# A two-layer transformer block with sorted experts: clearing fewer rows of the sorted array, on another queue

## What is computed

```
xn = layernorm(x)
x  = x + linear_attention(xn) + moe16(xn)     # 16 experts of 176, every token weighed over its best 6
xn = layernorm(x)
x  = x + recurrence(xn) + moe8(xn)            # scan of 512 steps: s = tanh(u_t + s*gamma + beta)
                                              # 8 experts of 176, best 2 per token, and 2 shared experts
```

## Time and profile before

| | |
|---|---|
| time, median of 3 | 658.88 us (658.23 to 660.16) |
| profiled execution: span, first to last instruction | 655.6 us |
| median less span | 3.3 us |
| TensorE busy | 610.9 us, 93% of the span |
| VectorE, ScalarE, GpSimd busy | 447.3, 366.1, 239.1 us |
| DMA: moved, written to HBM | 97.99 MB, 63.24 MB |

### The profile page before, as it was taken

One profiled execution on the slowest core, in us unless ns is written; L12 is line 12 of the kernel. 1 busy time (PEld: TensorE's weight loads), 2 busy tenths in 40 slices (PEclk: granted clock), 3 DMA queues, 4 the chain that ended last, 5 costly groups with the idle time before them and its releaser, 6 DMA issues. The chain is left out here.

```text
span 655.6 us, 12530 instructions
## 1 busy us (share of the span) xinstructions
PE 610.9 (93%) x3579; PEld 338.7 (52%) x3579; DVE 447.3 (68%) x1526; ACT 366.1 (56%) x1004; POOL 239.1 (36%) x256
## 2 busy tenths in 40 slices
PE   5999899999999999999999989999979989777997
PEld 2665444544444444444454434454446667556675
DVE  7983967667862677776478696477676666676677
ACT  2446345456546446657755657754546765663561
POOL 5246222132242225524224533222542361374371
PEclk8999999999999999999999999999998999999999
DMA  8203667872386452855346650324512445563143
GB/s 298 80 1 105 224 222 252 274 237 78 112 325 216 140 185 84 270 194 192 127 155 202 217 179 30 128 94 71 112 51 66 101 135 115 129 174 110 66 129 97
DMA packets 89548, 97.99 MB, mean 149 GB/s; under 512 B 29375, under 2 KB 80159, under 8 KB 89055
## 3 DMA queue, kind: packets, MB, share of 16 engines
q10 hardware_dynamic: 45472, 46.01, 21.4%
q1 hardware_dynamic: 38734, 36.82, 19.1%
q0 software_dynamic: 5280, 14.42, 7.0%
HBM read 27.96 MB, written 63.24 MB: 139 GB/s over the span
## 5 line engine op out<-in xcount | busy, mean ns | idle before, releaser
L1984 POOL TENSOR_TENSOR hl<-scr,hh 128x512 f16<-128x512 f32 (+2 forms) x91 | 105.3, 1157 | 276.6 <-ACT hh L1336 276.6
L1368 ACT ACTIVATE RING<-zbuf 128x16 f32<-128x16 f32 x512 | 110.9, 217 | 148.5 <-DVE zbuf L1830 143.5
L762 PE MATMUL G<-xT,W 128*128 128x512 f16 (+2 forms) x600 | 145.9, 379 | 8.2 <-ACT scr L1328 5.7
L762 PE MATMUL U<-xT,W 128*128 128x512 f16 (+2 forms) x600 | 145.8, 379 | 2.8 <-DVE scr L1845 2.8
L1830 DVE TENSOR_TENSOR_SCAN zbuf<-C,RING 128x32 f32<-128x32 f32 x354 | 77.8, 220 | 75.0 <-ACT RING L1368 74.6
L762 PEld LDWEIGHTS U<-xT,W 128*128 128x128 f16 (+3 forms) x600 | 60.9, 102 | 71.9 <-DVE scr L1845 4.3
L762 PEld LDWEIGHTS G<-xT,W 128*128 128x128 f16 (+3 forms) x600 | 60.1, 102 | 73.1 <-issue 6.4
L1020 PE MATMUL Y<-hh,W 128*128 128x512 f16 x352 | 90.3, 379 | 0.0
L1851 DVE TENSOR_TENSOR U<-U,CS 128x512 f32<-128x512 f32 x88 | 60.4, 686 | 38.6 <-PE U L762 31.9
L1328 ACT ACTIVATE scr<-G 128x512 f32<-128x512 f32 (+2 forms) x100 | 58.9, 589 | 45.0 <-PE G L762 44.5
L1336 ACT ACTIVATE hh<-scr 128x512 f16<-128x512 f32 (+2 forms) x100 | 61.8, 618 | 29.1 <-DVE scr L1845 28.9
(11 more groups left out here) (204 smaller groups left out, 839.5 us busy)
## 6 DMA issues: line engine op xcount, KB each, us to landing
xrows<-zeros ACTq DMA_DIRECT2D x13, 1280.0 KB, 5.7
yrows<-zeros ACTq DMA_DIRECT2D x10, 1536.0 KB, 6.0
stage<-weights SPq DMA_DIRECT2D x20, 384.0 KB
yrows<-zeros ACTq DMA_DIRECT2D x5, 1408.0 KB, 6.0
yrows<-scr POOLq DMA_DIRECT2D x46, 128.0 KB
xrows<-zeros ACTq DMA_DIRECT2D x5, 1152.0 KB, 5.4
stage<-weights SPq DMA_DIRECT2D x14, 256.0 KB
parked<-RING SPq DMA_DIRECT2D x1, 3520.0 KB, 12.0
```

The costliest lines, as they stand in the source:

```text
L762: last = nc.tensor.matmul(bank_, w(wp), act(ap), start=start and n == 0, stop=stop and n == count - 1)
L1368: nc.scalar.activation(RING[:, (t + 1) % RING_T, ::2], zbuf[:, 1::2], ACT.Tanh).then_inc(state_done, 1)
L1984: nc.gpsimd.tensor_tensor(hl[rows, a, :], h32[a][rows, :], hh[rows, a, :], ALU.subtract)\
```

## The change

`xrows` is no longer cleared whole. At the start of phase 0 ScalarE issues two DMAs that clear the idle tiles of both groups. CAP becomes 1152, so that 128 rows behind an expert's last row always lie in its region. When a group's `seen` is final, VectorE copies it as integers (`end_row`), and SyncE reads the eight row numbers one by one into a register and clears 128 rows from each: for group 0 between parking the weights and bringing them back, for group 1 ahead of the loads of pair 11. `load_tiles` waits for both clears, `scatter` for none. Larger regions make `yrows` larger too (191 tiles of 128 rows, not 175); its clearing stays.

```diff
-CAP = 2 * COLS
+CAP = 2 * COLS + P
-FILL_PARTS = (18, 15)
+FILL_PARTS = 15
...
-                for k in range(PAIRS):
-                    front[k].append(("fill", (0, k)))
+                front[0].append(("clear_idle", ()))
...
-                if phase == 1:
-                    for k in range(FILL_PARTS[0] - PAIRS):
-                        front[3 + k].append(("fill", (0, PAIRS + k)))
...
+            def clear_ends(group):
+                sp.wait_ge(ends_known, group + 1)
+                for e in range(E1):
+                    row = sp.value_load(end_row[0:1, group, e:e + 1], min_val=P, max_val=ROWS - P)
+                    sp.dma_start(xrows[DS(row, P), :], zeros.bitcast(f16)[:, :]).then_inc(ends_cleared, 16)
+
             def load_tiles(r):
                 group = group_of_pair(r)
                 if r == 0 or group > group_of_pair(r - 1):
+                    if r:
+                        clear_ends(group)
+                    sp.wait_ge(x_filled, 16 * len(GROUPS))
+                    sp.wait_ge(ends_cleared, 16 * E1 * (group + 1))
                     sp.wait_ge(table_done, 2 * (group + 1))
                     sp.wait_ge(scattered, 16 * K1 * BATCH * len(GROUPS[0]) * (group + 1))
...
             park(1, SHARED_PIECE, spare[0:HF, SPARE_DOWN_AT:2 * SPARE_DOWN_AT])
+            clear_ends(0)
             bring_back(0, 10, 0, P)
...
+            def clear_idle():
                 act.wait_ge(zeros_made, 1)
+                for g in range(len(GROUPS)):
+                    first = P + g * REGION + E1 * CAP
+                    nc.scalar.dma_start(xrows[first:first + TILES * P, :].rearrange("(n p) d -> p n d", p=P),
+                                        zeros.bitcast(f16)[:, :].unsqueeze(1).broadcast_to([P, TILES, 2 * DIM]))\
+                      .then_inc(x_filled, 16)
...
                 if part == 0:
+                    nc.vector.tensor_copy(end_row[one, group, :], seen[one, :]).then_inc(ends_known, 1)
...
             def scatter(j, b):
-                pool.wait_ge(filled[0], 16 * FILL_PARTS[0])
```

More of the change, by code:

```diff
@@ L166, in build @@
         tile_expert = sb("tile_expert", [P, len(GROUPS), TILES], i32)
+        end_row = sb("end_row", [P, len(GROUPS), E1], i32)
         ident, mask = cst[:, 0:P], cst[:, P:2 * P]
@@ L284, in build @@
         xr_tail = sem("xr_tail")
-        filled = [sem("x_filled"), sem("y_filled")]
+        x_filled, y_filled = sem("x_filled"), sem("y_filled")
+        ends_cleared = sem("ends_cleared")
         sorter_made = sem("sorter_made")
@@ L291, in build @@
         table_done = sem("table_done")
+        ends_known = sem("ends_known")
         scattered = sem("scattered")
@@ L390, in stages @@
                 front[SCATTER].append(("scatter", (phase - 1, 0)))
-                if phase == 1:
-                    for k in range(FILL_PARTS[0] - PAIRS):
-                        front[3 + k].append(("fill", (0, PAIRS + k)))
-                for part in range(FILL_PARTS[1]):
+                for part in range(FILL_PARTS):
                     if part // PAIRS == phase - 2:
-                        front[part % PAIRS].append(("fill", (1, part)))
+                        front[part % PAIRS].append(("fill", (part,)))
                 if phase == 2:
@@ L1279, in spread, with fill @@
                 nc.scalar.activation(spread_slot(phase), bank_[:, :], ACT.Copy).then_inc(spread_copied, 1)
-            def fill(n, part):
-                rows, empty = ((xrows, zeros.bitcast(f16)), (yrows, zeros.bitcast(f32)))[n]
-                first, end = (ROWS // P * (part + more) // FILL_PARTS[n] for more in (0, 1))
-                act.wait_ge(zeros_made, 1)
[L1286 to L1290, removed]
+            def fill(part):
+                first, end = (ROWS // P * (part + more) // FILL_PARTS for more in (0, 1))
+                nc.scalar.dma_start(yrows[first * P:end * P, :].rearrange("(n p) d -> p n d", p=P),
+                                    zeros.bitcast(f32)[:, :].unsqueeze(1).broadcast_to([P, end - first, DIM]))\
+                  .then_inc(y_filled, 16)
+            def clear_idle():
+                act.wait_ge(zeros_made, 1)
+                for g in range(len(GROUPS)):
[3 more added lines that the diff above has]
+                      .then_inc(x_filled, 16)
+            share = {"fill": fill, "clear_idle": clear_idle, "spread": spread, "norm_turn": norm_turn, "exp": exp, "cw_turn": cw_turn, "query": query,
                      "o_turn": o_turn, "rows": rows,
@@ L2047, in store_tiles @@
                 if r == 0:
-                    pool.wait_ge(filled[1], 16 * FILL_PARTS[1])
+                    pool.wait_ge(y_filled, 16 * FILL_PARTS)
                 rows = tiles_of(tile_row)
```

## The result

| | before | after |
|---|---|---|
| median, 4 runs each | 658.56 us (656.37 to 660.16) | 663.07 us (662.53 to 664.98) |
| span of the profiled execution | 655.6 us | 660.9 us |
| TensorE busy | 610.9 us | 615.5 us |
| written to HBM | 63.24 MB | 50.53 MB |

The ratio is 1.0082, with a 95% interval of 1.0057 to 1.0108. The change makes the kernel slower, by 4.5 us in the medians and 5.3 us in the spans. The forecast of no difference was wrong, and 663.07 lies above its range. The traffic fell as forecast: 12.7 MB less. The quotient of the two medians, 1.0068, lies inside the interval. One run of e1 (1283.83 us) and one of e2 (907.72 us) were far slower than all others; the ratios of the experiments leave them out, the medians do not.

The account below looks back on a forecast made before the run. TensorE, busy 93% of the span, was taken as the bound. Fills 0, burst 0, copies 0.1 and wait 0 gave a span of 655.7 us, with 3.3 us to the median 659.0; range 657.0 to 661.5.

Parts of the forecast that it names:

- forecast of no difference: Whole kernel: 659.0 us, within 0.3% (2.0 us) of the kernel before; chance 0.75.
- two end by 56.9, and the SiLU starts at 57.48: 0: ScalarE, start of phase 0: both idle clears are issued before the first SiLU, at most 0.43 us for one; cost 0.
- the burst starves the weights: Phase 0, rival: weight pieces queue behind the two idle clears, ScalarE and TensorE 2.3 us late, 661.3 us; chance 0.05.
- 1.05, between the two nearest: SyncE, group 1: each of eight clears takes 1.05 us (bounds 0.93 and 1.79), so pair 11's loads start 1.6 us later.
- cover behind pair 12: Pairs 11 to 13: SiLU comes well after the product, so a delay moves the end only by what exceeds 2.9 us.
- one after the other: SyncE, group 1, rival: clears run in turn at 2.4 us each, loads 11.1 us late, 667.1 us; chance 0.02.
- The removed fills: First array's fills: TensorE hardly feels the removed traffic, 12.7 MB less written net; counted 0.
- The clears of group 0, the copies and the loops: SyncE's group 0 clears: 0; VectorE's two copies: 0.1 us; ScalarE's three loops, in waits for TensorE: 0.
- SyncE holds up the second group: Group 1, rival: clears dearer than 1.52 us each delay pair 11's loads, up to 662.8 us; chance 0.10.
- deciding point of 4.9 us: Group 1: delay of the loads beyond which the kernel counts as slower, 2.9 us of cover plus 2.0.

Follow-up runs that it names:

- e1: Changed kernel with the second idle clear moved from the start of phase 0 to its sixth pair (pair 5); 660.97 us, 1.0047 of the kernel before.
- e2: Changed kernel with the second idle clear issued at the same moment by SyncE instead of ScalarE; 664.58 us, 1.0089 of the kernel before.
- e4: Changed kernel with the second idle clear at pair 5 and the row numbers copied earlier, in the group's last place; 657.03 us, 0.9991 of before.
- e5: Changed kernel with the two idle clears cut into six pieces at the same place on ScalarE; 669.32 us in one run, before 655.56.
- e8: Changed kernel with row numbers copied earlier and the second idle clear at pair 5 in three pieces; 655.96 us, one run.
- e3: Changed kernel with the row numbers copied earlier, in the group's last place step instead of the table's first; 661.18 us, 1.0048 of before.
- e6: Changed kernel with SyncE reading all eight row numbers of a group first, then issuing the eight clears; 663.48 us, 1.0091 of before.

## Why the prediction was wrong

**The step that failed first: "two end by 56.9, and the SiLU starts at 57.48: 0".** It priced an issue at the longest of 18 issues, 0.43 us. Those of phase 0 stand 7 to 11 us apart (56.00, 63.11, 73.44 and so on), and a fill lands in 5.9 us at the median, so that the one before was mostly down. One fill took 14.4 us to land (issued at 189.04), and the next one was issued beside it in 0.38 us; but that was about 1.2 MB, issued 11 us earlier. None shows an issue right behind 3.0 MB. For the clears of group 1, whose price the trace does not show either, the prediction took a bound from each side; here it took only the lower one. An upper bound was the time of the transfer ahead: 3.0 MB at 352 GB/s, 8.6 us. It measured 4.71 us for the issue, a wait of 3.72 us for TensorE, 1.7 us more at the lower clock and 2.05 us given back: 3.4 us in place of 0. The landmark shows 2.97 of them, in part because phase 0 had begun 0.24 us earlier (55.56 instead of 55.80). e1 took exactly this step back and returned 0.35%.

**The rival "the burst starves the weights"** had the right place and the wrong mechanism. The prediction asked whether two queues share the DMA engines evenly, answered yes, and forecast the pieces 4.5 us after they were asked for, the burst's end at 73.5 and no wait. The wait was as forecast (0.19 us at most for these pieces, 0.23 for the next), the way there was not: the pieces took 8.0 us, 4.8 of them without a packet, and the burst lasted until 77.7 (56.54 + 21.2 us to landing). ScalarE took the first piece 7.5 us after it was asked for, so nothing was to spare, and that part of the 0 was luck. The prediction did not ask what the burst does to the engine that issues it. e2 shows the same hold on SyncE, and there it does make the weights late.

**The second step: a clear costs "1.05, between the two nearest".** The first read came at 530.7, less 2.97 is 527.7, where 527.6 was forecast. The clears were 1.26 us apart, within the bounds of 0.93 and 1.79. Of the 1.26 a read takes 0.46 and an issue 0.33 at the median; the other 0.47 us are the steps on registers around the two. The prediction took 0.60 for the read with its steps, from a place where the two reads took 0.27 and 0.26 themselves, and 0.33 for the issue, and left 0.12 for the rest. That makes seven gaps 1.5 us longer. Two smaller terms were not in the sum: 0.3 us more between the end of the wait and the first load (1.54 us where it was 1.21), and the first transposing issue, 2.03 us instead of 1.19. Pair 11's loads were 3.7 us late where 1.6 was forecast, and pair 12's second was there 4.6 us late.

**What held.** The cover behind pair 12 was read as 2.9 us. 4.6 - 2.9 = 1.7 us, and ScalarE's four waits add up to 2.0. The step on the clears "one after the other" was rightly given little: they overlap, with 1.9 us to land and 1.26 between them. The removed fills were worth 0, as forecast, as far as e4's interval can tell. The clears of group 0, the copies and the loops cost nothing: with both causes taken away the time is that of before. The rival "SyncE holds up the second group" was the right mechanism too, and its deciding point of 4.9 us was not reached, at 4.6: alone, its 2.0 us lie at the bound of 0.3% (e1: 0.47%, from 0.26 to 0.69). It is the first step, for whose mechanism there was no rival, that carried the time out of the range.

## What to carry to other kernels

An issue of a DMA was cheap here only with little under way on its own queue (0.42 us alone, 4.71 right behind 3.0 MB): price it from a row that was issued behind as much as it will be, and put large transfers apart, or on an engine and at a place that has nothing to do next. Merging the fills of phase 0 into two transfers at one place turned issues worth 0 into one of 4.7 us on the engine that the next product waits for. Where a list of short steps is put into a wait, take each step's whole slot from start to start, and start the list as soon as its data is there, not where the code that uses it stands.

## What the runs showed that was not expected

- An issue can hold its engine for longer than any activation of that stretch: 4.71 us behind 23 tiles, and up to 3.00 us for a piece of 7 tiles behind five others. On SyncE a weight piece of 0.4 MB, asked for 9 us after a clear of 23 tiles, took 4.29 us to issue (e2). What counts is the own queue: beside a clear on the other one, SyncE's issues took 0.39 us (e2, the clear) and 0.35 and 0.74 us (the changed kernel, the two weight pieces). What the limit counts stays open: in e5 the last three issues ended when three pieces (3.0 MB) were left, yet the changed kernel's second issue ended at 61.25, while the first clear landed only at 55.77 + 10.6 = 66.4, and e8's third ended at 102.6, with none of its three pieces down (the first landed at 105.6).
- A wait of 3.72 us was followed by products at a granted clock of 0.50, which added 1.7 us to it. It was so behind each of the other long waits too (e2, e3, e5: a product of 2.77, 2.72 and 2.72 us). The waits of 1.64 us did not show this: the products behind them took 1.47.
- Reading eight numbers in a row and issuing eight DMAs in a row was no faster on SyncE than doing the two in turn: 1.3 and 1.26 us for each pair, in one trace of e6, where two of the issues were long.
- The first transposing load behind the clears was issued in 2.03 us. Such issues aren't tied to the clears: the other slot's 24 loads of the kernel before reach 3.04 us at a median of 1.20, and in e3 both of pair 11's took 1.2. What makes one long was not tried.
